# Attention with expert routing beside it: slots of routed tokens placed in six pieces in bodies 5 and 7, in place of three lumps in bodies 4 and 6

## The chip, the cores and the metric

The kernel runs as one program on 1 core of one Trainium2 chip. The metric is the time on the device in microseconds (us); lower is better. Engines: PE is TensorE (matmuls; PEld are its weight loads), DVE is VectorE, ACT is ScalarE, POOL is GpSimd, and SP is the queue of the sync engine, which here starts most of the DMAs.

## The reference, cut to what matters

Eight sequences of 512 tokens with 128 channels pass through six layers.

```python
x = L0_attn_x                                    # (8, 512, 128)
x = x + 0.5 * _L0_ffn_ref(_layernorm(x), ...)    # 8 experts, top 2: phase moe0, first time
x = x + _L0_attn_ref(_layernorm(x), ...)         # phase attn
x = x + 0.5 * _L0_ffn_ref(_layernorm(x), ...)    # moe0, second time
x = x + 0.5 * _L1_ffn_ref(_layernorm(x), ...)    # 16 experts, top 2: moe1
x = x + _L1_attn_ref(_layernorm(x), ...)         # state space: ssm
x = x + 0.5 * _L1_ffn_ref(_layernorm(x), ...)    # moe1

# _L0_attn_ref: 16 heads of 8 channels, softmax over 512 keys
attn = softmax(einsum('bhqd,bhkd->bhqk', q, k) * scale)
out = einsum('bhqk,bhkd->bhqd', attn, v)

# _L0_ffn_ref: which two experts a token goes to
logits = xf @ w_router
topk_w, topk_idx = top_k(softmax(logits), 2)
```

The change is in the attention phase, and in the routing for the mixture behind it, which is worked out beside attention.

## The kernel before

Each engine has its program written out by hand, and semaphores tie them. The phase of attention (`attn_phase`) runs eight *bodies*, one for each sequence b. A body has 16 steps, `st`, each with two *units*; the number of a unit, `at = 2 * st + j`, runs from 0 to 31. In a unit TensorE makes one tile of transposed scores of two heads (`st_pe`, L2227) in a pair of PSUM banks, and ScalarE takes its exponential (`exp_act`, L2235). In the same unit TensorE makes the tile of scores that is 16 units ahead (`max_pe`, L2159), and VectorE takes its maximum over the keys (`max_dve`, L2167). Both kinds of tile go through three PSUM pairs in turn. In each step comes the product with the values too (`av_pe`, L2245).

Other work stands between the units at fixed places, in order on each engine. On VectorE `between_dve` has: outputs divided by their sums (`o_dve`, L2267 and L2269) at units 6, 14, 22 and 30, the residual of the sequence before (`z_dve`, L2297) at 10, statistics for the router at 11 and 12 (L435, L444), v with its bias at 18 (L1911, up to body 5), and up to body 4 eight pieces of the combining of the previous mixture's outputs (L324) and the statistics of a later sequence. On TensorE `turn_pe` has work that shares PSUM bank 7, so that each piece waits until what the one before it left there has been read: among it the projections of q (unit 1, L1812), k (unit 15, L1817) and v (unit 17, L1823) of sequence b + 2, the transposes of the split maxima, `mT_pe` (L2203, units 3, 11, 19 and 27), and the transposes for the norm of sequence b + 3 in the last unit (L1831).

GpSimd (`pool_b`) splits the maxima of four heads into three bf16 parts (`msplit_pool`, L2191 to L2195), which `mT_pe` waits for. It splits q and k of sequence b + 2 (`split_pool`, L1902 to L1906), takes the root for the router's norm (`seq_root`, L451 to L456), starts gathers of the previous mixture's rows (`gather_one`, L277, bodies 0 to 3), and *sends*: indirect DMAs that scatter normalized token rows into the experts' slots in HBM (`group_send`, L635). The pace of these DMAs is a wait on the number of finished exponentials.

The next mixture needs a slot for each token and each of its two experts. This goes by groups: group 0 is sequences 1 and 2, group 1 is 3 and 4, group 2 is 5 and 6. For each, VectorE picks the experts (`pick_a`, `pick_b`), TensorE counts positions (`group_pos`), ScalarE copies them (`group_copy`, L513), and VectorE places (`place_a`, `place_b`, `place_c`). Picking and placing are chains of small operations of 8 to 168 elements a partition, and each waits for the one before it. One table sets where they stand:

```python
late = {"pick_a": (0, 13), "pick_b": (0, 14), "pos": (1, 0), "place_a": (1, 5), "place_b": (1, 6), "place_c": (1, 7)}
GROUP_STEPS = ((3, late), (5, late), (7, last_body))
```

The first number is added to the group's body, the second is the step; `route_dve` runs them at the step's end. So group 0 is picked in steps 13 and 14 of body 3, counted in step 0 of body 4, and placed in units 11, 13 and 15 of body 4; group 1 likewise in bodies 5 and 6. Group 0's 16 sends follow in bodies 4 and 5 and group 1's in 6 and 7, in each body four behind the split of k and four at the end.

## Time and profile before

| what | value |
| --- | --- |
| time, median of 3 runs | 1492.95 us (1492.89 to 1493.4) |
| profiled execution, its own time | 1504.16 us |
| its span, first to last instruction | 1502.4 us |
| PE, DVE, ACT, POOL busy | 1298.2, 1153.1, 888.8, 522.2 us |
| chain that ended last | PE 58%, DVE 22%, issue 8%, ACT 6% |
| attention, first to last exponential | 322.9 to 739.8 us |
| bodies 0, 1, 2, 3 | 50.4, 53.6, 49.7, 52.8 us |
| bodies 4, 5, 6, 7 | 62.3, 50.4, 53.5, 44.2 us |
| L2167, maximum of a tile | 256 of them, mean 1218 ns |
| L2235, exponential of a tile | 256 of them, mean 1022 ns |

A body's length is from its first exponential to that of the next body. The profile is of one execution. Busy matmuls overlap, so a busy TensorE is not one at its peak. The granted clock is a share of 2.4 GHz; TensorE has two levels, 1.2 and 2.4 GHz, so 0.5 means the lower one throughout.

### The profile page before, as it was taken

What the parts mean: (1) busy time and instruction counts of PE and PEld (TensorE: products, weight loads), DVE (VectorE), ACT (ScalarE), POOL (GpSimd) and SP (SyncE); (2) the same over time, 40 slices, a digit from 0 to 9 for tenths busy, and PEclk for the clock granted to TensorE, in tenths of its full rate; (3) what the DMA queues carried; (4) which work ended last, traced back from release to release, by engine and by line L of the source; (5) the groups of instructions that cost most, each with busy time, mean ns of one, the idle gap of its engine ahead of it and who ended that gap; (6) DMA issues with size and microseconds to landing.
All of it is one profiled execution on the core that took longest, in us unless ns stands there. A gap on an engine that the chain in (4) does not pass through costs nothing.

```text
span 1502.4 us, 20416 instructions
## 1 busy us (share of the span) xinstructions
PE 1298.2 (86%) x6496; PEld 777.0 (52%) x6496; DVE 1153.1 (77%) x2430; ACT 888.8 (59%) x1402; POOL 522.2 (35%) x757
## 2 busy tenths in 40 slices
PE   3589999778899879979678999989999889889998
PEld 3467778522222212312256777766666444666665
DVE  5757979789989979898446989878786663787875
ACT  4567667348778858867666677633343465434432
POOL 6664326354534524522243334523430120201100
PEclk9989999869989989989989999999999998999999
DMA  8151264332212202210061122163543011055344
GB/s 298 50 136 61 91 210 148 114 105 84 88 42 88 84 29 75 87 36 23 16 252 50 49 71 91 57 149 92 122 106 79 13 28 25 1 114 115 78 93 113
DMA packets 88679, 133.94 MB, mean 89 GB/s; under 512 B 16756, under 2 KB 42836, under 8 KB 87548
## 3 DMA queue, kind: packets, MB, share of 16 engines
q1 hardware_dynamic: 81404, 117.93, 27.5%
q0 software_dynamic: 7168, 14.69, 3.2%
q8 instruction: 53, 0.87, 0.2%
q14 instruction: 54, 0.44, 0.1%
HBM read 82.23 MB, written 47.45 MB: 86 GB/s over the span
## 4 chain that ended last, share of the span: by engine, by line
PE 58%; DVE 22%; issue 8%; ACT 6%; DMA 3%; SPq 2%; POOL 0%; another core or an unknown queue 0%; DVEq 0%; ACTq 0%; POOLq 0%
PE bank L1557 6%; PE pair L894 5%; DVE shared L2167 5%; PE pair L896 5%; PE pair L895 5%; PE bank L2245 5%; PE pair L1469 3%; PE pair L1471 3%; PE pair L1470 3%; PE pair L2227 3%; PE pair L2159 3%; DVE shared L950 3%; ACT shared L2235 2%; PE bank L964 1%; DMA shared<-p_coef_rows 1%
## 5 line engine op out<-in xcount | busy, mean ns | idle before, releaser
L2167 DVE TENSOR_REDUCE shared<-pair 128x2 f32<-128x1024 f32 x256 | 310.0, 1218 | 45.4 <-PE pair L2159 41.9
L2235 ACT ACTIVATE shared<-pair 128x1024 f32<-128x1024 f32 x256 | 260.6, 1022 | 60.6 <-PE pair L2227 58.3
L950 DVE TENSOR_TENSOR shared<-shared 128x512 fp32r<-128x512 f32 x232 | 195.5, 851 | 91.7 <-ACT shared L940 56.7
L894 PE MATMUL pair<-shared 128*128 128x512 f32 x464 | 201.0, 433 | 12.6 <-issue 8.7
L1524 ACT ACTIVATE shared<-pair 128x512 f32<-128x512 f32 x144 | 85.6, 595 | 179.1 <-PE pair L1471 168.8
L896 PE MATMUL pair<-shared 128*128 128x512 f32 x464 | 189.4, 408 | 0.0
L895 PE MATMUL pair<-shared 128*128 128x512 f32 x464 | 189.0, 407 | 0.0
L935 ACT ACTIVATE shared<-pair,shared 128x512 f32<-128x512 f32 x168 | 115.9, 690 | 74.2 <-PE pair L896 68.6
L1469 PE MATMUL pair<-shared 128*128 128x512 f32 x288 | 153.8, 534 | 5.1 <-DVE shared L1479 5.1
L635 POOL DMA_INDIRECT xs_rows<-shared,slots x112 | 118.2, 1055 | 85.0 <-issue 24.6
L2245 PE MATMUL bank<-shared 128*9 128x512 f32 x1024 | 140.4, 622 | 4.5 <-ACT shared L2235 3.7
L277 POOL DMA_INDIRECT staged<-ys_rows,slots x112 | 118.1, 1054 | 58.9 <-ACT shared L2235 32.3
L1536 DVE TENSOR_TENSOR shared<-shared,pair 128x512 f32<-128x512 f32 x128 | 87.1, 682 | 58.8 <-ACT shared L1524 53.9
L1557 PE MATMUL bank<-shared,down_w 128*128 128x512 f32 x256 | 129.0, 595 | 1.9 <-DVE shared L1545 1.9
L2159 PE MATMUL pair<-shared 48*128 48x512 bf16 x512 | 105.0, 409 | 20.7 <-ACT shared L2235 9.9
L1471 PE MATMUL pair<-shared 128*128 128x512 f32 x288 | 114.9, 399 | 0.0
L1470 PE MATMUL pair<-shared 128*128 128x512 f32 x288 | 114.4, 397 | 0.0
L2227 PE MATMUL pair<-shared 51*128 51x512 bf16 x512 | 103.0, 400 | 12.9 <-DVE shared L2167 11.8
L894 PEld LDWEIGHTS pair<-shared 128*128 128x128 f32 x464 | 92.3, 199 | 32.4 <-issue 14.9
L2227 PEld LDWEIGHTS pair<-shared 51*128 51x128 bf16 x512 | 24.8, 93 | 159.7 <-issue 92.3
L896 PEld LDWEIGHTS pair<-shared 128*128 128x128 f32 x464 | 91.2, 196 | 22.0
L895 PEld LDWEIGHTS pair<-shared 128*128 128x128 f32 x464 | 92.7, 200 | 17.1 <-issue 0.2
(380 smaller groups left out, 2282.0 us busy)
## 6 DMA issues: line engine op xcount, KB each, us to landing
shared<-p_coef_rows SPq DMA_DIRECT2D x64, 512.0 KB
shared<-xs_rows SPq DMA_DIRECT2D x42, 256.0 KB
ys_rows<-shared SPq DMA_DIRECT2D x42, 256.0 KB
w_keep<-shared SPq DMA_DIRECT2D x8, 1024.0 KB
shared<-w_keep SPq DMA_DIRECT2D x16, 512.0 KB
shared<-p_q_parts SPq DMA_DIRECT2D x64, 96.0 KB
shared<-p_k_parts SPq DMA_DIRECT2D x64, 96.0 KB
xs_rows<-shared SPq DMA_DIRECT2D x1, 5376.0 KB, 18.4
```

Source lines behind the costliest of these rows:

```text
L894: nc.tensor.matmul(out_bank, w_hi, x_hi, start=start, stop=False)
L895: nc.tensor.matmul(out_bank, w_hi, x_lo, start=False, stop=False)
L896: return nc.tensor.matmul(out_bank, w_lo, x_hi, start=False, stop=stop)
L950: nc.vector.tensor_tensor(hl[u % RING][:], hid[u % RING][:], hh[u % RING][:], ALU.subtract).then_inc(s["dve_done"], 1)
L1469: nc.tensor.matmul(out_bank, w_hi, x_hi, start=start, stop=False)
L1470: nc.tensor.matmul(out_bank, w_hi, x_lo, start=False, stop=False)
L1471: return nc.tensor.matmul(out_bank, w_lo, x_hi, start=False, stop=stop)
L1557: nc.tensor.matmul(bank[6][:], w, h, start=(j == 0), stop=(j == IT - 1)).then_inc(s["down_done"], 1)
L2167: nc.vector.tensor_reduce(mneg[:, i, 2 * c:2 * c + 2], pair_of("max", b, m)[:], AX_X, ALU.max, negate=True).then_inc(s["mx_read"], 1)
L2227: last = nc.tensor.matmul(pair_of("exp", b, 2 * st + p)[:, f, :], ka[par][rows, c, kt * P:(kt + 1) * P], qa[par][rows, c, :], start=True, ...
L2235: nc.scalar.activation(probs[st % 2][:, 2 * p:2 * p + 2, :], pair_of("exp", b, 2 * st + p)[:], ACT.Exp, scale=scale).then_inc(s["exp_done" ...
L2245: last = nc.tensor.matmul(bank[6][32 * hh:32 * hh + HD + 1, :], v_all[:, b * TILES + kt, hh % 2 * (H // 2) + g * HG // 2 + hh // 2, :], pr ...
```

## The change

Placing moves to body 5 (group 0) and body 7 (group 1), into the first third of the body, in six pieces: `place_a`, `place_b` and `place_c` get an argument `half`, and `between_dve` runs the halves at units 3, 4, 5, 7, 8 and 9. Picks and counts come one body later. The sends of group 0 are spread over bodies 5 and 6 in twos, those of group 1 over body 7 in fours, at new places in GpSimd's order. Group 2 and the last sequence stay as they were. The lists of step names (`PE_STEPS`, `ACT_STEPS`, `DVE_STEPS`), from which the values of the waits are counted, follow the new order.

```diff
-        def place_a(v, occ, G):
+        def place_a(v, occ, G, half=None):
...
+            if half == 0:
+                return
             before = upto_e[1 - G % 2][:, NE0 - 1:NE0] if G else 0.0
...
-        def place_b(v, occ, G):
+        def place_b(v, occ, G, half=None):
...
+            if half == 0:
+                return
             chain(nc.vector.tensor_tensor(q, r, s1, ALU.mult))
...
-        def place_c(v, occ, G):
+        def place_c(v, occ, G, half=None):
...
+            if half == 0:
+                return
             chain(nc.vector.tensor_tensor(past_e[:], upto_e[G % 2][:].unsqueeze(1).to_broadcast([P, NBLK, NE0]),
...
-            late = {"pick_a": (0, 13), "pick_b": (0, 14), "pos": (1, 0), "place_a": (1, 5), "place_b": (1, 6), "place_c": (1, 7)}
+            late = {"pick_a": (0, 13), "pick_b": (0, 14), "pos": (1, 0)}
+            PLACED_IN = {5: 0, 7: 1}
+            PLACE_AT = {3: (place_a, 0), 4: (place_a, 1), 5: (place_b, 0), 7: (place_b, 1), 8: (place_c, 0), 9: (place_c, 1)}
...
-            GROUP_STEPS = ((3, late), (5, late), (7, last_body))
+            GROUP_STEPS = ((4, late), (6, late), (7, last_body))
...
+                if routed and b in PLACED_IN and at in PLACE_AT:
+                    place, half = PLACE_AT[at]
+                    place(v, routes, PLACED_IN[b], half)
                 if routed and at == 11:
...
-                sends = routes is not None and b > 3
-
-                def send(half):
-                    group_send(g, routes, (b - 4) // 2, 2 * (b % 2) + half, 4, lambda k, n: paced(b, 4 * half + k, 8))
+
+                def send(G, part, parts, at, every):
+                    if routes is not None:
+                        group_send(g, routes, G, part, parts, lambda k, n: g.wait_ge(s["exp_done"], PER * b + min(PER, int(at + every * k))))
...
+                if b == 6:
+                    send(0, 4, 8, 2, 2)
                 msplit_pool(g, b, 2)
                 fetch((3, 9))
                 xbo_pool(b)
                 if routes is not None and b:
                     seq_root(g, routes, b - 1)
                 fetch((4, 12))
+                if b == 5:
+                    send(0, 0, 8, 10, 1)
+                if b == 6:
+                    send(0, 5, 8, 11, 2)
+                if b == 7:
+                    send(1, 0, 4, 10, 1.5)
                 if b + FIRST < B:
                     split_pool(g, "q", b + FIRST)
                 fetch((5, 15))
+                if b == 5:
+                    send(0, 1, 8, 14, 1)
                 msplit_pool(g, b, 3)
                 if b + FIRST < B:
                     split_pool(g, "k", b + FIRST)
                 fetch((6, 20))
-                if sends:
-                    send(0)
+                if b == 5:
+                    send(0, 2, 8, 20, 2)
+                if b == 6:
+                    send(0, 6, 8, 18, 2)
+                if b == 7:
+                    for part in range(1, 4):
+                        send(1, part, 4, 12 + 5 * part, 1.25)
                 if not last_:
                     msplit_pool(g, b + 1, 0)
                 if b + AHEAD < B:
                     shift_a(f0 + b + AHEAD)
                 fetch((7, 27))
-                if sends:
-                    send(1)
+                if b == 5:
+                    send(0, 3, 8, 27, 2)
+                if b == 6:
+                    send(0, 7, 8, 27, 2)
```

Lines have other numbers after the change: the maximum L2167 is L2179, `o_dve` L2267 and L2269 are L2279 and L2281, `place_b` L598 to L606 is L603 to L613, `split_pool` L1902 to L1906 is L1912 to L1916, `msplit_pool` L2191 to L2195 is L2203 to L2207, and a send, L635, is L645.

VectorE, body 4 before, units 13 and 14: `place_b` of group 0 in one lump between two maxima (L2167), behind a piece of the combining (L324).

```order
L2167 TENSOR_REDUCE shared<-pair 128x2
L324 SCALAR_TENSOR_TENSOR x_res<-staged,w_tok,x_res 128x128
L598 TENSOR_TENSOR q_g<-pos_g,room_e 128x64
L599 TENSOR_TENSOR q_g<-q_g,jump_e 128x64
L600 TENSOR_TENSOR r_g<-pos_g,next_e 128x64
L601 TENSOR_TENSOR r_g<-r_g,q_g 128x64
L602 TENSOR_TENSOR q_g<-r_g,s_g 128x64
L603 TENSOR_REDUCE slot_f<-q_g 128x8
L604 TENSOR_TENSOR q_g<-r_g,sel_all 128x64
L605 TENSOR_REDUCE slot_f<-q_g 128x8
L606 CAST slots<-slot_f 128x16
L2167 TENSOR_REDUCE shared<-pair 128x2
```

VectorE, body 5 after, units 4 to 7: the end of `place_a`, the maximum of unit 5 (L2179), and `place_b` in two halves, with two maxima and `o_dve` between them.

```order
L593 TENSOR_TENSOR jump_e<-jump_e,next_e 128x8
L2179 TENSOR_REDUCE shared<-pair 128x2
L603 TENSOR_TENSOR q_g<-pos_g,room_e 128x64
L604 TENSOR_TENSOR q_g<-q_g,jump_e 128x64
L605 TENSOR_TENSOR r_g<-pos_g,next_e 128x64
L606 TENSOR_TENSOR r_g<-r_g,q_g 128x64
L2179 TENSOR_REDUCE shared<-pair 128x2
L2279 RECIPROCAL shared<-bank 128x16
L2281 TENSOR_TENSOR shared<-bank,shared 128x4x32
L2179 TENSOR_REDUCE shared<-pair 128x2
L609 TENSOR_TENSOR q_g<-r_g,s_g 128x64
L610 TENSOR_REDUCE slot_f<-q_g 128x8
```

The lump of nine operations has become a piece of four and one of five (the last three of it stand behind these rows), and it stands eight units earlier in the next body.

GpSimd, body 5 before, behind the statistics of unit 12: the end of `seq_root` (L456), the split of q, the maximum split of the body's last four heads, and the start of the split of k.

```order
L456 TENSOR_TENSOR sh_all<-sh_all,rs_all 128x4
L1902 CAST shared<-shared 128x512
L1903 TENSOR_TENSOR shared<-shared 128x512
L1904 CAST shared<-shared 128x512
L1906 TENSOR_TENSOR shared<-shared 128x512
L2191 CAST shared<-shared 128x8x2
L2192 TENSOR_TENSOR shared<-shared 128x16
L2193 CAST shared<-shared 128x8x2
L2195 TENSOR_TENSOR shared<-shared 128x8x2
L1902 CAST shared<-shared 128x512
```

GpSimd, body 5 after, the same place (L645 is a send):

```order
L456 TENSOR_TENSOR sh_all<-sh_all,rs_all 128x4
L645 DMA xs_rows<-shared,slots 10752x128 x2
L1912 CAST shared<-shared 128x512
L1913 TENSOR_TENSOR shared<-shared 128x512
L1914 CAST shared<-shared 128x512
L1916 TENSOR_TENSOR shared<-shared 128x512
L645 DMA xs_rows<-shared,slots 10752x128 x2
L2203 CAST shared<-shared 128x8x2
L2204 TENSOR_TENSOR shared<-shared 128x16
L2205 CAST shared<-shared 128x8x2
L2207 TENSOR_TENSOR shared<-shared 128x8x2
L1912 CAST shared<-shared 128x512
```

Two sends have come between `seq_root` and the split of q, and two more between that and the maximum split.

GpSimd, body 7 before: the end of `seq_root`, the maximum split of the last four heads, and eight sends.

```order
L456 TENSOR_TENSOR sh_all<-sh_all,rs_all 128x4
L2191 CAST shared<-shared 128x8x2
L2192 TENSOR_TENSOR shared<-shared 128x16
L2193 CAST shared<-shared 128x8x2
L2195 TENSOR_TENSOR shared<-shared 128x8x2
L635 DMA xs_rows<-shared,slots 10752x128 x8
```

GpSimd, body 7 after, the same place:

```order
L456 TENSOR_TENSOR sh_all<-sh_all,rs_all 128x4
L645 DMA xs_rows<-shared,slots 10752x128 x4
L2203 CAST shared<-shared 128x8x2
L2204 TENSOR_TENSOR shared<-shared 128x16
L2205 CAST shared<-shared 128x8x2
L2207 TENSOR_TENSOR shared<-shared 128x8x2
L645 DMA xs_rows<-shared,slots 10752x128 x12
```

Four sends now stand ahead of the maximum split, and twelve behind it.

## Rows read from the trace of the kernel before

**Rows 1.** Stretches, L2235 alone: span, length, busy (instructions), granted clock, DMA; units 12 to 19.

```profile
444.70:457.80 13.10, 8.18 (x9) 1.00 0.30 97
551.50:573.30 21.80, 8.21 (x9) 0.84 0.19 59
609.40:622.20 12.80, 8.18 (x8) 1.00 0.31 94
660.70:678.80 18.10, 8.18 (x8) 0.81 0.09 30
```

**Rows 2.** Stretches, L2235 alone: last units of bodies 2, 3; first units of 2, 4.

```profile
470.90:476.60 5.70, 4.01 (x4) 1.00 0.26 83
520.60:529.40 8.80, 4.03 (x4) 0.87 0.18 54
426.90:432.80 5.90, 4.10 (x5) 1.00 0.04 11
529.40:539.60 10.20, 4.10 (x4) 0.61 0.01 2
```

**Rows 3.** Stretches of VectorE: place_a (body 4), the lumps (body 6), units 3 to 9.

```profile
552.44:554.29 1.85, 1.43 (x11) 1.00 0.10 14
...
661.57:663.08 1.51, 1.27 (x9) 1.00 0.03 8
665.61:667.96 2.35, 2.04 (x10) 1.00 0.00 0
670.72:672.69 1.97, 1.70 (x9) 0.50 0.00 0
596.37:606.65 10.28, 8.93 (x9) 1.00 0.15 41
700.82:711.14 10.32, 8.93 (x10) 1.00 0.01 3
```

**Rows 4.** Timeline of bodies 4 and 6: start, length, engine, line, operation, [idle before <-releaser].

```profile
558.56 1.15 POOL L1903 TENSOR_TENSOR shared<-shared 128x512 f32<-128x512 f32 x1
558.59 1.20 DVE L602 TENSOR_TENSOR q_g<-r_g,s_g 128x64 f32<-128x64 f32 x1
...
666.73 0.22 DVE L602 TENSOR_TENSOR q_g<-r_g,s_g 128x64 f32<-128x64 f32 x1
```

**Rows 5.** Timeline of TensorE, bodies 4, 5, 6 and 7.

```profile
555.57 0.39 PE L2227 MATMUL pair<-shared 51*128 51x512 bf16 x2 [1.90 <-DVE shared L2167]
...
563.46 2.08 PE L1817 MATMUL bank<-xnT,w_k 128*128 128x512 f32 x2 [5.76 <-DVE shared L2269]
...
614.58 1.12 PE L1817 MATMUL bank<-xnT,w_k 128*128 128x512 f32 x2 [0.79 <-DVE shared L2269]
...
617.72 1.16 PE L1823 MATMUL bank<-w_v,xnT 128*128 128x128 f32 x8
...
621.33 0.39 PE L2203 MATMUL bank<-identb,shared 128*12 128x128 bf16 x4 [0.40 <-DVE shared L1911]
...
669.33 0.39 PE L2227 MATMUL pair<-shared 51*128 51x512 bf16 x2 [2.85 <-DVE shared L2167]
...
723.14 0.39 PE L2203 MATMUL bank<-identb,shared 128*12 128x128 bf16 x4
```

**Rows 6.** Timeline of GpSimd, bodies 5 and 7.

```profile
613.71 0.20 POOL L456 TENSOR_TENSOR sh_all<-sh_all,rs_all 128x4 f32<-128x4 f32 x1
...
617.55 0.21 POOL L2191 CAST shared<-shared 128x16 bf16<-128x16 f32 x1
...
618.41 0.22 POOL L2195 TENSOR_TENSOR shared<-shared 128x16 bf16<-128x16 f32 x1
...
622.51 1.12 POOL L635 DMA_INDIRECT xs_rows<-shared,slots  x1 [0.17 <-issue]
623.93 0.97 POOL L635 DMA_INDIRECT xs_rows<-shared,slots  x1 [0.30 <-issue]
...
718.18 0.20 POOL L456 TENSOR_TENSOR sh_all<-sh_all,rs_all 128x4 f32<-128x4 f32 x1
```

More of the change, by code:

```diff
@@ L568, in pick_dense @@
             v.wait_ge(rs_["dve_step"], dve_at(occ, "pkd"))
-        def place_a(v, occ, G):
+        def place_a(v, occ, G, half=None):
             ts, nt, b = group(occ, G)
             chain = route_chain(v)
-            v.wait_ge(rs_["act_step"], act_at(occ, f"p{G}"))
+            if half != 1:
+                v.wait_ge(rs_["act_step"], act_at(occ, f"p{G}"))
             counts = pos_g[:, NE0 * nt:NE0 * (nt + 1)]
             upto = upto_e[G % 2]
-            if G == 0:
+            if G == 0 and half != 1:
                 chain(nc.vector.memset(next_e[:], 0.0))
@@ L613, in place_c @@
             counts = pos_g[:, NE0 * nt:NE0 * (nt + 1)]
-            chain(nc.vector.scalar_tensor_tensor(out=moved_e[:], in0=rest_e[:], scalar=0.0, in1=jump_e[:], op0=ALU.is_gt, op1=ALU.mult))
-            chain(nc.vector.tensor_tensor(next_e[:], next_e[:], counts, ALU.add))
-            chain(nc.vector.tensor_tensor(next_e[:], next_e[:], moved_e[:], ALU.add))
-            chain(nc.vector.scalar_tensor_tensor(out=room_e[:], in0=blocks_e[:], scalar=float(T), in1=rest_e[:], op0=ALU.mult, op1=ALU.subtract))
+            if half != 1:
+                chain(nc.vector.scalar_tensor_tensor(out=moved_e[:], in0=rest_e[:], scalar=0.0, in1=jump_e[:], op0=ALU.is_gt, op1=ALU.mult))
+                chain(nc.vector.tensor_tensor(next_e[:], next_e[:], counts, ALU.add))
+                chain(nc.vector.tensor_tensor(next_e[:], next_e[:], moved_e[:], ALU.add))
+                chain(nc.vector.scalar_tensor_tensor(out=room_e[:], in0=blocks_e[:], scalar=float(T), in1=rest_e[:], op0=ALU.mult, op1=ALU.subtract))
+            if half == 0:
+                return
             chain(nc.vector.tensor_tensor(past_e[:], upto_e[G % 2][:].unsqueeze(1).to_broadcast([P, NBLK, NE0]),
```

26 lines of the change are left out of this document (13 added, 13 removed).

## The prediction

> **What bounds the kernel now.** I read the busy shares and the chain of waits on the page first, then the stages of the attention phase cut at its Exp instructions, then the timeline inside them. "Body b" is the loop body of attention that computes the scores of sequence b; its 32 "units" are its 32 Exp instructions, and beside unit u VectorE reduces a maximum 16 units ahead (L2167, 1.22 us each, in the table of the profile). An Exp tile and a maximum tile share three PSUM pairs, so when VectorE is late, the tile of a later Exp is late too. ScalarE has slack. In a body without routing work the chain of waits alternates between TensorE and VectorE, and neither has much to give: eight units or nine take 11 to 13 us.
>
> The small routing work is what breaks the rhythm. Units 12 to 19 take 13.1 us in body 2, which has no placing, and 21.8 us in body 4, where the lumps of group 0 stand at units 11, 13 and 15 [rows 1]. That is 8.7 us of excess. For group 1 in body 6 the same units take 18.1 us. Body 6 projects no k and v; body 5 does, and takes 12.8 us. Of that the k projection (1.12 us on TensorE [rows 5]) certainly falls away and the v projection (1.16 us) partly, so the base of body 6 is 10.5 to 11.7 us; I take 11.1, and the excess is 7.0 us. The picks with the position counts behind them cost too: the last four units of body 3 take 8.8 us against 5.7 in body 2, and the first four of body 4 take 10.2 against 5.9 [rows 2], together 7.4 us.
>
> **What the lumps are made of.** The three lumps last 1.51, 2.35 and 1.97 us in body 6 [rows 3], 5.83 us in sum. In body 4 place_a takes 1.85 us (it has three memsets more). Its place_b is slower than body 6's, since single operations are stretched: L602 takes 1.20 us there, with GpSimd's L1903 of the split of q running at the same moment, and 0.22 us in body 6, where no split runs [rows 4]. The Trainium skill, GPSIMD Engine Reference, section Key points, says that GpSimd shares its SBUF interfaces with VectorE and contends with VectorE instructions that have two SBUF inputs. The trace agrees (1.20 against 0.22 us). By that rule units 3 to 9, where only the four short operations of a maximum split run on GpSimd, are free of it, which is also what I assume from the rows. So in the new place group 0 costs 1.85 + 2.35 + 1.97 = 6.17 us and group 1 5.83 us of VectorE. The rest of the excess is idle TensorE: gaps of 5.76 us in body 4 and 2.85 us in body 6, and after each a stretch in which TensorE runs at its lower clock (1.2 GHz): k's pair of matmuls takes 2.08 us where body 5 needs 1.12 [rows 5].
>
> **Part 1: the lumps go.** Saved: 8.7 (body 4) + 7.0 (body 6) = 15.7 us.
>
> **Part 2: six pieces in units 3, 4, 5, 7, 8, 9 of bodies 5 and 7.** From the maximum of unit 3 to that of unit 10 VectorE is busy 8.93 of 10.28 us in body 5 and 8.93 of 10.32 us in body 7 [rows 3], so 1.35 and 1.39 us are free. No piece is longer than 1.25 us, so a piece goes into a gap and the buffer behind it, not in front of a standing TensorE. But 6.17 us of work go into 1.35 us of room: slip 6.17 - 1.35 = 4.8 us in body 5 and 5.83 - 1.39 = 4.4 us in body 7. Directly behind follow z_dve, the statistics and their aggregation (units 10 to 12), where VectorE has no idle time to catch up. Bounds: 0 (all of it beside TensorE, which is what the chain runs through up to unit 9) and 12.0 us for both (none hidden). I stay with 9.2, since in bodies 4 and 6 nothing of the lumps was hidden.
>
> **Part 3: the sends.** A send is one indirect DMA on GpSimd's queue, about 1.12 us for the first and 0.97 for the next with 0.30 between [rows 6]. Their number is the same (32), but what stands behind them is not. In body 5 two sends now stand between seq_root and the split of q, and two more between that and the maximum split of group 3 (see the order of GpSimd's instructions). That split feeds mT(5,3), which TensorE takes up in unit 19, in order. Today seq_root ends at 613.91, the split of q follows without a gap, the maximum split ends at 618.63, and TensorE starts the transposes at 621.33, having waited 0.40 us for VectorE: 2.7 us of room [rows 5, 6]. Each pair of sends adds 0.17 + 1.12 + 0.30 + 0.97 = 2.56 us, two pairs 5.1. All four are past their pace by then (Exp 10, 11, 14, 15 are done). So the split ends at 623.75 and TensorE stands 2.4 us longer. Queued behind on TensorE are all later Exp and maximum tiles, so ScalarE and VectorE stand too. Behind the split on GpSimd stand the split of k, two sends and the next maximum split, which has some 5 us until its maximum is read; nobody waits there. In body 7 four sends stand between seq_root (ends 718.38) and the maximum split: 718.38 + 0.17 + 1.12 + 3 x 0.30 + 3 x 0.97 = 723.5, and 1.08 for the split (617.55 to 618.63 in body 5) gives 724.6, against transposes that start at 723.14 today: 1.4 us. In body 6 two sends stand there; the split has to wait for its maximum about as long anyway: 0. Sum 3.8 us, bounds 0 and 4.
>
> **Part 4: clock.** TensorE's clock fell after idle 5.76 and 2.85 us but not after the single 1.90 us [rows 5]. In body 5 the gap in unit 19 would be 0.40 + 2.4 = 2.8 us, so I expect a short fall there: the work behind it (Exp, maximum and AV tiles, about 0.9 us a unit at 2.4 GHz) doubles for a few units that have half a microsecond of room each; I take 1.0 us, and 0.3 in body 7, where the gap is shorter. Bounds 0 and 6.4: at worst the clock is low from the pieces on, and the 4.9 us of TensorE on body 5's chain from k to the tiles of unit 19 double, with 1.5 us in body 7.
>
> **Part 5: picks and positions move one body on.** Group 0's go from the end of body 3 and start of body 4 to the end of 4 and start of 5. The norm transposes behind the pick (b + 3 < 8) and the q projection behind the positions (b + 2 < 8) are there too, so the 7.4 us move and stay. Group 1's go from bodies 5/6 to 6/7, neither of which has those. I price it at 0, with 1 us to both sides. The fillers of body 4 that the old sends stood among gain nothing, since no engine waits for those. The last send is due at Exp 30 as before, so the MoE phase behind starts unchanged.
>
> **Sum.** -15.7 + 9.2 + 3.8 + 1.3 = -1.4 us. The profiled execution took 1504.16 us (span 1502.4), which is 11.2 us more than the median of the timed runs, 1492.95; the excess lies on all phases, so I carry the difference over unchanged: 1491.5 us.
>
> **Rivals.**
> 1. GpSimd isn't late. If the sends cost its queue less than their rows, or if the pieces' slip leaves the statistics no later while v of unit 18 is, the 3.8 us and the clock's 1.3 go: -6.5 us, 1486.5. For it: today one gather stands at each of the two places in bodies 0 to 3, and nobody waits. Against it: 2.7 us of room hold one pair, not two.
> 2. The slip is not hidden at all (12.0), all else as forecast: +1.4 us, 1494.3, no measurable change. For it: the lumps were paid in full. Against it: 1.35 us of idle time are in the rows.
> 3. Slower, by one mechanism: TensorE's clock. Pieces between all maxima thin out TensorE from unit 3 on; if the clock falls there and is still low when k and v are projected in units 15 to 17, 6.4 us stand in place of 1.3: +3.7 us, 1496.6. It decides from about 3 us of low clock on TensorE's part of the chain. For it: 0.61 was granted in the first units of body 4 [rows 2], right before where the pieces now would be in body 5. Against it: in bodies 4 and 6 it came back as soon as the lumps were over.
> 4. The same work in the same amounts is merely moved, and each place costs what the old one did: 0.
>
> **Chances.** Forecast 0.42, rival 1 0.25, rival 2 and 4 together 0.18, rival 3 0.15. A measurement of this kernel tells about 0.2% (3 us) from no change, that is 1490.0 and 1495.9. Faster: rival 1 nearly whole (0.23) and a third of the forecast's spread (0.13), 0.36. Slower: most of rival 3 (0.12) and tails of the rest (0.10), 0.22. Within: 0.42. Range: from rival 1 to rival 3, 1486.5 to 1496.6; beside it, the forecast's own is 1489 to 1494.
>
> **What would show it.** In the profile after: units 12 to 19 of bodies 4 and 6 back near 13.1 and 11.1 us; units 3 to 10 longer by 4.8 and 4.4 us in bodies 5 and 7, with VectorE without idle time and pieces at their uncontended durations; a wait of TensorE of about 2.8 us before the transposes of unit 19 in body 5, released by GpSimd, and one of 1.4 us in body 7; an end of body 4 and a start of body 5 like those of 3 and 4 before. No wait there means rival 1; k at 2.08 us in body 5 means rival 3. I am wrong altogether if places that I call unchanged (body 3, or what follows attention) move by more than 1 us.

## The result: no gain where a small one was forecast, and slower in the first measurement

| kernel | median us | runs | ratio to before | 95% interval |
|---|---|---|---|---|
| changed, first measurement | 1506.9 (before 1492.95) | 5 | 1.0093 | 1.0055 to 1.0131 |
| changed, again | 1496.65 | 12 | 1.0012 | 0.9985 to 1.0039 |
| changed, third time | 1498.72 | 12 | 1.0019 | 0.9985 to 1.0053 |

The forecast was 1491.5 us, range 1486.5 to 1496.6. The first measurement is 15 us above it, and the other two lie at the upper end of the range and above it. They put the kernel 2.5 and 4.8 us above the medians of before that were taken beside them (1494.16 and 1493.95), which the ratios can't tell from none. The ratios leave out single slow runs (one, of kernel 7 below, took 2446 us) and are not quotients of the medians. Otherwise a kernel's runs spread over 9 to 26 us, so the lengths of the bodies in the traces are the sharper measure. Those below repeat within 2 us for one kernel; in the pieces-only kernel body 4 differed by 2.8 us between two profiles. Most of that lies in the first three units behind group 0's picks, which take 5.7 to 8.9 us and differ by 2 to 3 us between profiles of one kernel; the units behind them are steadier. I read the bodies as before, from Exp to Exp (L2247 now; other lines of attention have moved by 10 or 12 too: the maximum is L2179, AV L2257, mT's transposes L2215, the split's last operation L2207, a send L645).

| us | body 3 | 4 | 5 | 6 | 7 | sum |
|---|---|---|---|---|---|---|
| before, first and second profile | 52.8, 52.2 | 62.3, 60.5 | 50.4, 50.4 | 53.5, 52.7 | 44.2, 44.2 | 263.2, 260.0 |
| changed, three profiles | 49.7, 49.7, 49.7 | 51.8, 51.4, 52.0 | 60.4, 60.4, 61.1 | 49.1, 49.1, 49.1 | 55.2, 56.4, 56.6 | 266.2, 267.0, 268.5 |

The change takes 10 us from body 4 and 4 from body 6 and puts 10 us on body 5 and 11 to 12 on body 7. The stretches that answer to [rows 1] and [rows 2], ScalarE's L2247 alone (stretch, length, busy (instructions), granted clock, DMA share, GB/s): units 12 to 19 of bodies 2, 4 and 6; units 19 to 21 of body 5 and 22 to 31 of body 7; the last units of body 4 and first of 5, and the last of body 3.

```profile
442.80:455.90 13.10, 8.20 (x9) 1.00 0.32 99
542.10:555.20 13.10, 8.17 (x8) 1.00 0.30 93
654.90:666.30 11.40, 8.16 (x8) 1.00 0.17 54
...
612.30:622.30 10.00, 3.07 (x3) 0.67 0.45 138
722.90:740.80 17.90, 10.05 (x10) 0.71 0.11 37
567.50:576.20 8.70, 4.03 (x5) 0.92 0.16 48
576.20:584.40 8.20, 4.07 (x4) 0.88 0.00 0
518.60:524.40 5.80, 4.05 (x5) 1.00 0.29 83
```

Body 4 reads like body 2, and body 6 needs 11.4 us where it needed 18.1. The picks' 19.0 us of two stretches [rows 2] have moved by one body and take 16.9, with a higher clock in the second. That is no gain of the change: the first four units behind the picks took 10.2 and 8.3 us in the two profiles of before (body 4) and 8.3, 9.5 and 10.3 us in the three after it (body 5). VectorE in units 3 to 11 of bodies 5 and 7, which took 13.3 us before (see [rows 3] for units 3 to 9):

```profile
583.00:601.00 18.00, 16.47 (x39) 0.91 0.09 23
690.10:708.30 18.20, 16.31 (x36) 0.81 0.01 2
```

It is busy 92% and 90% of the time, and the units take 17.9 and 18.2 us. TensorE does wait for VectorE here, as in unit 7 of body 5, and its clock falls for a while (0.91 and 0.81 granted over the two stretches):

```profile
591.59 0.89 PE L2288 MATMUL bank<-ident,shared 128*128 128x128 f32 x4 [2.22 <-DVE shared L2281]
```

The waits that answer to [rows 5]: TensorE in unit 19 of body 5 and what follows (start, us, engine, line, operation, [idle before <-releaser]).

```profile
612.12 0.38 PE L2171 MATMUL pair<-shared 48*128 48x512 bf16 x2
616.29 0.59 PE L2215 MATMUL bank<-identb,shared 128*12 128x128 bf16 x4 [3.79 <-POOL shared L2207]
...
617.78 1.90 PE L2257 MATMUL bank<-shared 128*9 128x512 f32 x8
```

TensorE waits 3.79 us for GpSimd's split, and at its lower clock (1.2 GHz; 0.67 granted over the three units) an AV tile then takes 1.90 us instead of 1.05. Now body 7, which holds the larger part of the miss. GpSimd first, from the split for unit 19 on (compare [rows 6]), then ScalarE, then TensorE:

```profile
719.03 0.22 POOL L2207 TENSOR_TENSOR shared<-shared 128x16 bf16<-128x16 f32 x1
719.74 1.01 POOL L645 DMA_INDIRECT xs_rows<-shared,slots  x1 [0.49 <-issue]
721.05 0.96 POOL L645 DMA_INDIRECT xs_rows<-shared,slots  x1 [0.30 <-issue]
722.32 0.96 POOL L645 DMA_INDIRECT xs_rows<-shared,slots  x1 [0.30 <-issue]
...
728.62 0.96 POOL L645 DMA_INDIRECT xs_rows<-shared,slots  x1 [0.31 <-issue]
```

```profile
725.87 1.03 ACT L2247 ACTIVATE shared<-pair 128x1024 f32<-128x1024 f32 x1
728.97 0.58 ACT L2264 COPY shared<-bank 128x512 f32<-128x512 f32 x1 [2.06 <-remote]
729.71 1.02 ACT L2247 ACTIVATE shared<-pair 128x1024 f32<-128x1024 f32 x1 [0.15 <-remote]
```

```profile
719.39 0.38 PE L2215 MATMUL bank<-identb,shared 128*12 128x128 bf16 x4 [1.83 <-POOL shared L2207]
...
725.13 1.05 PE L2257 MATMUL bank<-shared 128*9 128x512 f32 x8 [0.21 <-ACT shared L2247]
...
727.42 0.39 PE L2239 MATMUL pair<-shared 51*128 51x512 bf16 x2
730.78 1.90 PE L2257 MATMUL bank<-shared 128*9 128x512 f32 x8 [2.97 <-issue]
```

Eight sends stand in one row, 1.26 us from start to start (six in the two later profiles). ScalarE's L2264 wants the AV tile, which TensorE had done at 726.18 by the trace; it starts at 728.97, and the trace names no releaser ("remote"). TensorE waits for ScalarE in turn, and its clock falls. Units 22 to 31 take 18.0 us against 12.5 before. What the late signal is, the experiments had to say.

### The profile page after: what moved, and what is told of

The parts are those of the page before. It is cut to its first block, busy times and chain, and to the rows that moved or that the text cites. A ratio compares the mean times of both kernels' runs of the same rounds, so it can differ in the third digit from the quotient of the medians.

```text
span 1503.5 us, 20427 instructions
## 1 busy us (share of the span) xinstructions
PE 1293.0 (86%) x6496; PEld 775.9 (52%) x6496; DVE 1152.8 (77%) x2430; ACT 887.5 (59%) x1402; POOL 523.1 (35%) x757
## 4 chain that ended last, share of the span: by engine, by line
PE 54%; DVE 23%; issue 9%; ACT 7%; DMA 3%; SPq 2%; POOL 2%; another core or an unknown queue 1%; DVEq 0%; POOLq 0%; ACTq 0%
PE bank L1567 6%; PE pair L904 5%; PE pair L905 5%; PE pair L906 5%; PE bank L2257 5%; DVE shared L2179 5%; PE pair L1479 3%; PE pair L1481 3%; PE pair L1480 3%; PE pair L2239 3%; DVE shared L960 3%; PE pair L2171 3%; ACT shared L2247 2%; DMA shared<-p_coef_rows 1%; PE bank L974 1%
## 5 line engine op out<-in xcount | busy, mean ns | idle before, releaser
L2179 DVE TENSOR_REDUCE shared<-pair 128x2 f32<-128x1024 f32 x256 | 310.0, 1218 | 41.7 <-PE pair L2171 37.7
L2247 ACT ACTIVATE shared<-pair 128x1024 f32<-128x1024 f32 x256 | 260.3, 1021 | 55.9 <-PE pair L2239 52.2
L904 PE MATMUL pair<-shared 128*128 128x512 f32 x464 | 199.0, 429 | 11.2 <-issue 7.2
L905 PE MATMUL pair<-shared 128*128 128x512 f32 x464 | 187.6, 404 | 0.0
L645 POOL DMA_INDIRECT xs_rows<-shared,slots x112 | 119.0, 1063 | 79.3 <-issue 27.5
L2257 PE MATMUL bank<-shared 128*9 128x512 f32 x1024 | 140.8, 623 | 6.4 <-ACT shared L2247 3.3
L2171 PE MATMUL pair<-shared 48*128 48x512 bf16 x512 | 103.8, 403 | 22.3 <-ACT shared L2247 11.4
L1481 PE MATMUL pair<-shared 128*128 128x512 f32 x288 | 116.4, 404 | 0.0
L904 PEld LDWEIGHTS pair<-shared 128*128 128x128 f32 x464 | 91.3, 197 | 30.4 <-issue 13.2
L906 PEld LDWEIGHTS pair<-shared 128*128 128x128 f32 x464 | 90.6, 195 | 21.5
L905 PEld LDWEIGHTS pair<-shared 128*128 128x128 f32 x464 | 91.2, 197 | 16.7 <-issue 0.2
```

What stands on the lines that cost most here:

```text
L904: nc.tensor.matmul(out_bank, w_hi, x_hi, start=start, stop=False)
L905: nc.tensor.matmul(out_bank, w_hi, x_lo, start=False, stop=False)
L906: return nc.tensor.matmul(out_bank, w_lo, x_hi, start=False, stop=stop)
L1481: return nc.tensor.matmul(out_bank, w_lo, x_hi, start=False, stop=stop)
L2179: nc.vector.tensor_reduce(mneg[:, i, 2 * c:2 * c + 2], pair_of("max", b, m)[:], AX_X, ALU.max, negate=True).then_inc(s["mx_read"], 1)
L2247: nc.scalar.activation(probs[st % 2][:, 2 * p:2 * p + 2, :], pair_of("exp", b, 2 * st + p)[:], ACT.Exp, scale=scale).then_inc(s["exp_done" ...
```

## The experiments

All lines in the expectations count from the kernel they name. Each kernel was timed in 12 runs (one in 11), beside before on the same chip.

**1 and 2. Both kernels again.** No edit.

> The kernel before, unchanged, run against itself. It says how far two executions of one kernel lie apart, since the profiled execution of before took 1504.16 us and its timed runs 1490 to 1498. If the 14 us of the change are its own (theory 1), this ratio is 1.000 within 0.3% and its runs lie near 1493. If both kernels have a wide and common spread and the change only drew the worse part of it (theory 2), some of these runs lie at 1500 and above. In the profile I expect bodies 2, 3, 4, 5, 6, 7 of 49.7, 52.8, 62.3, 50.4, 53.5, 44.2 us again within 0.5 us where the clock is the same.

> The changed kernel, unchanged, as the reference of this group. Theory 1: ratio 1.007 to 1.011 again (about 1504 to 1509 us against 1493). Theory 2: a ratio under 1.005, since the attention phase of the one profile is only some 3 us longer than before's where the clock is alike. Both expect in the profile a wait of TensorE for GpSimd of 3 to 4 us in unit 19 of body 5 and 1.5 to 2 us in unit 19 of body 7.

Before took 1492.66 us, ratio 1.0018 to itself (0.9982 to 1.0053); the changed kernel took 1496.65, as theory 2 has it. The 14 us between the medians of the first measurement did not return. The bodies of the changed kernel did, and both waits of unit 19 (3.79 and 1.83 us). Those of before returned less well than the 0.5 us I expected: body 4 took 60.5 us instead of 62.3, body 6 52.7 instead of 53.5, and body 1, which the change does not touch, 49.7 instead of 53.6. The two profiles that belong to the first measurement are only 1.1 us apart in span (1502.4 and 1503.5 us), so no stretch of them can show the rest.

**3. The pieces alone.** The pieces in units 3 to 9 of bodies 4 and 6; picks, positions and sends as before.

```
-            late = {... "pos": (1, 0), "place_a": (1, 5), "place_b": (1, 6), "place_c": (1, 7)}
+            late = {"pick_a": (0, 13), "pick_b": (0, 14), "pos": (1, 0)}
+            PLACED_IN = {4: 0, 6: 1}
```

> One part of the change alone: the six pieces in units 3, 4, 5, 7, 8, 9, but in the old bodies 4 and 6, with the old picks, counts and sends. If the pieces are what is good in the change and the new places of the sends are what is bad (my account), bodies 4 and 6 get shorter by 3.9 and 2.6 us (8.7 and 7.0 of lumps go, 4.8 and 4.4 of slip come), nothing waits for GpSimd, and the time is 4 to 8 us under before's: 1485 to 1489, ratio 0.995 to 0.997. The rival, that pieces between all maxima cost more than lumps (TensorE's clock, or turns of bank 7 that wait for late VectorE), expects 1493 or more and units 3 to 12 of bodies 4 and 6 longer by over 8 us.

Measured 1489.2 us, ratio 0.9983 (0.9949 to 1.0017). Body 4 went from 60.5 us (before, second profile) to 56.5 and body 6 from 52.7 to 51.1. Run once more, unchanged:

> The kernel with the pieces only, unchanged, once more, to narrow its ratio (0.9983 of before, 0.9949 to 1.0017, the first time). If its bodies 4 and 6 gain 5.6 us as their lengths say, the ratio is 0.996 to 0.998; if that is given back elsewhere, 1.000.

1489.42 us, ratio 0.9969 (0.9947 to 0.9991). Here the bodies were 59.3 and 51.9 us, so the 5.6 us of the first profile did not return whole. Without the three units behind the picks the gain is steady: units 3 to 31 take 50.8 and 50.5 us in body 4, where before needs 53.5 and 53.6, and 45.8 and 46.0 us in body 6, where before needs 48.2 and 48.3. So six pieces do beat three lumps where the lumps stood, and the loss of the change is not in them.

**4. The sends of bodies 5 and 7 behind the split for unit 19.** The same calls ahead of the split are removed.

```
                 msplit_pool(g, b, 3)
...
                 fetch((6, 20))
                 if b == 5:
+                    send(0, 0, 8, 10, 1)
+                    send(0, 1, 8, 14, 1)
                     send(0, 2, 8, 20, 2)
...
                 if b == 7:
+                    send(1, 0, 4, 10, 1.5)
                     for part in range(1, 4):
```

> The changed kernel with the sends that stood ahead of the maximum split of unit 19 (four in body 5, four in body 7) put right behind it (body 5: behind the split of k), nothing else. My account: the waits of TensorE for GpSimd in unit 19 of bodies 5 and 7 (3.8 and 1.8 us) go with the fall of the clock behind the first, so attention is 5 to 8 us shorter than with the change, 1496 to 1502 us if the change takes 1507 here. If the long row of back-to-back sends in body 7 is what costs (its 16 sends now all come after unit 18, without a gap), units 20 to 31 of body 7 get longer than the 22.6 us they take with the change, and the gain is under 3 us. Rival, that the time is lost outside attention: no change against the changed kernel.

The gain did not come: 1504.78 us, ratio 1.0079 (1.0048 to 1.0109). Unit 19 did fall to 1.49 us in body 5 and 1.37 in body 7, as it should, but body 5 took 61.8 us and body 7 60.2. That is the second branch of the expectation, the long row: units 20 to 31 of body 7 took 25.6 us (20.6 in the changed kernel, not the 22.6 given there). The sends now stood in rows of six (615.0 to 621.5) and eleven (717.9 to 730.7). ScalarE in the second row:

```profile
724.42 1.02 ACT L2247 ACTIVATE shared<-pair 128x1024 f32<-128x1024 f32 x1 [0.88 <-PE pair L2239]
727.96 1.02 ACT L2247 ACTIVATE shared<-pair 128x1024 f32<-128x1024 f32 x1 [2.52 <-remote]
730.07 0.59 ACT L487 COPY shared<-bank 128x512 f32<-128x512 f32 x1 [1.08 <-remote]
731.54 1.02 ACT L2247 ACTIVATE shared<-pair 128x1024 f32<-128x1024 f32 x1 [0.89 <-PE pair L2239]
735.07 0.59 ACT L2264 COPY shared<-bank 128x512 f32<-128x512 f32 x1 [2.50 <-remote]
```

The Exp at 727.96 reads scores that TensorE had ready at 725.48. The trace also records when a semaphore is raised. Over attention that is 0.02 us after the end of TensorE's instruction in the median of 742. Here the score tile's signal is recorded at 727.93, 2.45 us late, and ScalarE starts 0.03 us after it; the AV tile done at 730.08 is signalled at 735.05, and ScalarE starts at 735.07. In body 5's row VectorE waits so too (1.43 and 1.69 us, "remote"). Hence theory A of the experiments that follow: in a row of sends the signals of other engines come late. Its rival B: an instruction fetch, or waits for mT. The traces speak against a fetch. In the changed kernel's first profile the nearest one of 16 KB lies ahead of the row, from 716.34 to 717.87, and none is recorded between 719.2 and 741 us in this one.

**5. The kernel before, with the eight sends of body 7 in one row.** Nothing else moves: same number of sends, same order on GpSimd.

```
-                nc.gpsimd.wait_ge(s["exp_done"], PER * b + 16 + 16 * k // n)
+                nc.gpsimd.wait_ge(s["exp_done"], PER * b + (20 if b == B - 1 else 16 + 16 * k // n))
```

> The kernel before, with one change: the eight sends of body 7 are all let go at unit 20 instead of two units apart, so that they stand in one row on GpSimd, some 1.27 us from start to start (before: 2.3 to 2.8 us apart; body 7 took 44.2 us in both profiles of this kernel). Theory A (late signals): while sends follow each other at 1.27 us, from the third or fourth on, TensorE's signals reach ScalarE late, as in the kernel with sends behind the split (ScalarE idle 2.52, 1.08 and 2.50 us 'remote' in a row of eleven). Eight in a row should then cost body 7 2 to 6 us: 46 to 50 us, with ScalarE waits put down to 'remote' of 0.5 us and more. Rival B (what was seen there was an instruction fetch or the waits for mT, and a row of sends costs the other engines nothing): body 7 stays at 44.2 within 0.5 us and no such wait appears; the sends then just end 5 us earlier. The time: A 1492.7 + 4 = 1497, B 1492.7.

1502.03 us, ratio 1.0054 (1.0029 to 1.0079). Body 7 went from 44.2 to 51.6 us, more than the 46 to 50 I gave theory A, and rival B falls. GpSimd, ScalarE, TensorE (its Exp is L2235, scores L2227, AV L2245):

```profile
723.55 1.12 POOL L635 DMA_INDIRECT xs_rows<-shared,slots  x1 [3.90 <-ACT shared L2235]
724.98 0.97 POOL L635 DMA_INDIRECT xs_rows<-shared,slots  x1 [0.30 <-issue]
...
732.57 0.96 POOL L635 DMA_INDIRECT xs_rows<-shared,slots  x1 [0.31 <-issue]
```

```profile
729.52 1.02 ACT L2235 ACTIVATE shared<-pair 128x1024 f32<-128x1024 f32 x1 [0.89 <-PE pair L2227]
732.38 0.59 ACT L2252 COPY shared<-bank 128x512 f32<-128x512 f32 x1 [1.84 <-remote]
733.79 1.02 ACT L2235 ACTIVATE shared<-pair 128x1024 f32<-128x1024 f32 x1 [0.83 <-remote]
```

```profile
727.94 1.04 PE L2245 MATMUL bank<-shared 128*9 128x512 f32 x8 [0.21 <-ACT shared L2235]
...
730.23 0.39 PE L2227 MATMUL pair<-shared 51*128 51x512 bf16 x2
734.87 1.89 PE L2245 MATMUL bank<-shared 128*9 128x512 f32 x8 [4.26 <-issue]
```

The signals are late from the fourth send on: 1.7 us for the score tile done at 727.73, 3.4 us for the AV tile done at 728.98. Up to the row the body is as before. The two stretches, up to unit 22 and from it on, all engines (PE, PEld, DVE, ACT, POOL busy (instructions), granted clock, DMA):

```profile
694.00:725.70 31.70, 26.97 (x204) 7.89 (x208) 22.75 (x32) 26.60 (x35) 7.35 (x19) 1.00 0.01 4
725.70:745.60 19.90, 13.84 (x77) 3.56 (x69) 3.73 (x15) 11.40 (x15) 6.01 (x7) 0.74 0.07 23
```

And the second of them in the repeat of before, where the sends stand 2.3 to 3.0 us apart:

```profile
717.30:729.80 12.50, 10.18 (x77) 3.21 (x69) 3.75 (x15) 10.86 (x15) 4.81 (x5) 1.00 0.08 27
```

The same 77 groups of matmuls take 3.7 us more at the lower clock, and the waits make up the rest of 7.4 us. The DMA engines are no busier than 8% in either. "Done" is the end that the trace gives, and ends of matmuls are modelled; but TensorE started its scores at 730.23, 2.1 us before the signal of the AV tile that it had finished ahead of them.

**6. The pieces alone, with gaps between the sends.** In bodies 4 and 5 the first four sends were due before GpSimd came to them and ran as a row of four, and so did the last four of body 4.

```
-                nc.gpsimd.wait_ge(s["exp_done"], PER * b + 16 + 16 * k // n)
+                nc.gpsimd.wait_ge(s["exp_done"], PER * b + (16 + 2 * k if b == B - 1 else min(PER, 20 + 2 * k)))
```

> The kernel with the pieces only (bodies 4 and 6, old sends), with the sends of bodies 4, 5 and 6 let go at units 20, 22, 24, 26, 28, 30, 32, 32 instead of 16, 18, 20, ... 30: there the first four were due before GpSimd came to them and ran in a row of four, 1.27 us apart (at 561.9, 575.3 and 612.4 us). Theory A (late signals in rows of sends): units 22 and 23 of body 5 come down from 1.94 and 1.96 to 1.6 each or less, body 4's units 19 and 22 from 2.20 and 2.38 to 1.6; bodies 4 and 5 together 106.9 -> 104 to 105.5 us, time 1489.2 -> 1487.5 (less than the measurement can tell). Rival B (rows cost nothing): these units as they are, and the time the same. If later sends hold up the next body's GpSimd work, body 5 or 6 gets longer by 1 to 3 us at its first units: that would be seen at units 0 to 3.

1487.99 us, ratio 0.9963 (0.9934 to 0.9991). Units 22 and 23 of body 5 fell from 1.94 and 1.96 to 1.50 and 1.65, as theory A has it, and unit 22 of body 4 from 2.38 to 1.51. Unit 19 of body 4 stayed at 2.21, so it had nothing to do with the sends, and unit 27 rose from 1.78 to 2.94. Bodies 4 and 5 together did not get shorter: 108.8 us against 106.9, with 2.4 us more in the first three units of body 4, ahead of all sends. In the second profile of kernel 3 they took 109.6 us, so this is the spread of those units. A row of four costs under 1 us, and the time does not show it.

**7. Four sends in body 5, twelve in body 6.**

```
                 msplit_pool(g, b, 3)
...
                 if b == 5:
-                    send(0, 2, 8, 20, 2)
+                    send(0, 0, 8, 21, 2)
...
                 if b == 5:
-                    send(0, 3, 8, 27, 2)
+                    send(0, 1, 8, 27, 2)
```

(and the first two calls in body 5 are gone; body 6 sends parts 2 to 7 in pairs from units 2, 8, 12, 19, 23 and 27.)

> The changed kernel with only four of group 0's sends in body 5 (at units 21, 23, 27, 29, all behind the split of the maxima for unit 19) and twelve in body 6, in pairs two units apart (it had eight and eight, four of them ahead of that split). Theory A (the four sends ahead of the split made mT late, the clock fell after it, and moving them behind it failed only because six then stood in a row): unit 19 of body 5 goes 5.19 -> 1.49, units 20 and 21 2.48 to 2.73 -> 1.36 and to 1.31, body 5 60.4 -> 55 to 56 us, body 6 49.1 -> 49 to 50; time 1496.65 -> 1491.5. Rival B (the work of twelve sends holds up GpSimd's splits in body 6 as it did in body 5): body 6 49.1 -> 52 or more, with waits for L2207 in front of TensorE, and the time stays at 1494 to 1497. Rival C (body 5 is long for the clock alone): body 5 stays at 58 or more.

1495.1 us, ratio 1.0003 (0.9977 to 1.0028), above the 1491.5 that theory A gave. The lengths follow theory A: units 19 to 21 took 4.15 us (as in before; 10.0 in the changed kernel), body 5 55.6, body 6 49.6. Body 7, untouched, took 57.4. TensorE's wait before mT is back to 0.41 us, for VectorE:

```profile
608.99 0.39 PE L2215 MATMUL bank<-identb,shared 128*12 128x128 bf16 x4 [0.41 <-DVE shared L1921]
```

**8. Eight sends in body 7, eight behind it.**

```
-                    send(1, 0, 4, 10, 1.5)
+                    send(1, 0, 8, 10, 2)
...
-                        send(1, part, 4, 12 + 5 * part, 1.25)
+                        send(1, part, 8, 16 + 4 * part, 2)
...
+                if b == 7:
+                    send(1, 1, 2, 32, 0)
```

> The changed kernel with only eight of group 1's sixteen sends in body 7, two units apart and six of them behind the split for unit 19; the other eight follow in a row after body 7's last exponential. Theory A (in body 7 the row of sends makes TensorE's signals late, and sends ahead of the split make mT late): unit 19 2.60 to 2.92 -> 1.37, units 22 to 29 lose the 4 to 5 us that they had over before; body 7 55.2 to 56.4 -> 49 to 51 us (44.2 before, and the pieces' slip of 5). Rival B (these units are slow for an instruction fetch that comes there anyway, or for the clock): body 7 stays at 53 or more. The eight sends in a row stand then where other work runs: what the stretch behind body 7 (to 830 us) pays is 0 if GpSimd is free there and up to 8 x 1.27 = 10 us if not; so the time is 1496.65 - 5.5 + (0 to 10) = 1491 to 1501, and only the body's length decides between A and B.

1496.13 us, ratio 0.9988 (0.9959 to 1.0018): alone, the mend of 7 us in body 7 does not show in the time beyond its noise. Body 7 took 49.0 us: unit 19 is 1.37 and units 22 to 31 take 12.5 us, exactly as before the change; what stays is the pieces' slip. GpSimd in two places:

```profile
722.63 1.01 POOL L645 DMA_INDIRECT xs_rows<-shared,slots  x1 [4.15 <-ACT shared L2247]
724.76 0.96 POOL L645 DMA_INDIRECT xs_rows<-shared,slots  x1 [1.12 <-ACT shared L2247]
...
746.88 0.96 POOL L645 DMA_INDIRECT xs_rows<-shared,slots  x1 [0.30 <-issue]
750.46 0.25 POOL L451 TENSOR_SCALAR sh_all<-mv_all 128x4 f32<-128x4 f32 x1 [2.62 <-DVE mv_all L430]
```

The row behind the body ends 2.6 us before GpSimd is wanted, and from the last Exp to the first matmul of L905 in the next stage it is 17.4 us, against 17.0. To the hundredth matmul of L904 it is 119.2 us, where kernels without such a row take 116.6 to 118.3.

**9. Both mends together** (7 and 8).

> The changed kernel with both edits of its sends at once: four of group 0's sends in body 5 behind the split, twelve in body 6; eight of group 1's in body 7 two units apart, eight behind its last exponential. Theory A (late signals in rows of sends, and sends ahead of the split, are what the changed kernel loses beyond the pieces' slip, and they add up): body 5 55.6 us, body 6 49.6, body 7 49.0, so that bodies 5 to 7 are 11 us shorter than in the second run of the changed kernel (165.9 -> 154 to 156), and the stretch behind pays nothing; time 1496.65 - 6 to 11 = 1486 to 1491. Rival B (what is gained there comes back as a lower clock elsewhere, as the runs of single mends gained only 1.6 and 0.5 us in the median): bodies 154 to 156, but the time stays at 1494 to 1497.

1487.17 us, ratio 0.9953 (0.9924 to 0.9982): faster than before and than the changed kernel. Bodies 5, 6 and 7 by stretch:

```profile
577.00:630.30 53.30, 45.93 (x327) 14.29 (x325) 46.44 (x77) 40.09 (x51) 17.32 (x33) 0.97 0.20 63
630.30:679.90 49.60, 41.82 (x314) 12.65 (x314) 44.28 (x63) 38.65 (x49) 18.19 (x33) 1.00 0.14 45
679.90:728.60 48.70, 40.11 (x280) 10.98 (x278) 31.23 (x71) 37.83 (x48) 13.41 (x25) 0.93 0.04 12
```

and in the changed kernel:

```profile
576.20:636.60 60.40, 49.62 (x327) 14.37 (x325) 46.55 (x77) 40.29 (x51) 20.90 (x36) 0.90 0.20 61
636.60:685.70 49.10, 41.96 (x314) 12.70 (x315) 44.28 (x63) 38.55 (x49) 14.29 (x29) 1.00 0.13 39
685.70:740.80 55.10, 43.11 (x280) 12.40 (x278) 31.09 (x71) 38.16 (x48) 21.03 (x33) 0.85 0.06 20
```

151.6 us against 164.6, with the same work on every engine but GpSimd (one weight load more or less in the records), and the time follows (rival B said it would not): the changed kernel beside it took 1498.72 us. Body 5 is shorter here than the 55.6 us expected because its first three units took 5.7 us, 8.1 in kernel 7; 1.1 of the 13 us between the two tables are of that kind.

**10. Group 1 placed where VectorE has no maxima.** Kernel 3, with group 1's pieces in units 17 to 22 of body 7 and its sends from unit 26 on, most of them behind the body.

```
+            PLACE_AT = {4: dict(zip((3, 4, 5, 7, 8, 9), HALVES)), 7: dict(zip((17, 18, 19, 20, 21, 22), HALVES))}
...
+                    group_send(g, routes, 1, pace=lambda k, n: g.wait_ge(s["exp_done"], PER * b + min(PER, 26 + 2 * k)))
```

> The kernel with the pieces only, but group 1's six pieces in body 7 at units 17 to 22, where VectorE has no maxima left to find, in place of body 6 at units 3 to 9; group 1's sends two units apart from unit 26 of body 7, most of the sixteen in a row behind its last exponential. Theory A (the slip of 5 us is VectorE's queue alone, so pieces cost nothing where no maximum stands behind them): body 6 51.1 -> 49 to 49.6, body 7 44.2 -> 44.2 to 45.5, stretch behind it (last exponential to the first matmul of the next stage 17.1 us) as before; time 1489.2 -> 1487.5. Rival B (twelve sends behind the last exponential hold up the next stage's own sends and its first loads of routed rows): that stretch grows by up to 12 x 1.27 = 15 us, and the time goes to 1495 to 1504. Rival C (VectorE is wanted there after all, by the picks and the copies of the last body): body 7 goes to 47 or more.

1486.12 us, the lowest median of all, ratio 0.9968 (0.9937 to 0.9999). Body 6 took 46.9 us (51.1 in kernel 3) and body 7 stayed at 44.2:

```profile
633.30:680.20 46.90, 43.28 (x315) 12.67 (x313) 41.97 (x50) 38.68 (x48) 6.32 (x21) 0.96 0.09 27
680.20:724.40 44.20, 37.10 (x277) 11.09 (x277) 31.43 (x71) 37.45 (x48) 8.53 (x20) 1.00 0.02 6
```

Body 6 is below the 49 to 49.6 us I expected; it lost its sends with its pieces, but its units 3 to 11 alone went from 17.5 us to 13.3, which is the whole difference. Pieces cost nothing where no maximum stands behind them in VectorE's queue, so the slip is that queue. From the last Exp to the first matmul of L905 it stays at 17.1 us; the hundredth matmul of L904 comes 120.4 us behind the last Exp, 117.3 in kernel 3. In kernel 9, with eight sends in that place, it is 116.4. Whether this or kernel 9 is the better one the intervals don't tell.

**11. The changed kernel a third time.**

> The changed kernel, unchanged, a third time (1.0093 the first time, 1.0012 the second). By the bodies of its two profiles (bodies 4 to 7 take 6 to 7 us more than before) it should be at 1.003 to 1.006; if the first measurement held for all chips, 1.009; if the second, 1.001.

1498.72 us, ratio 1.0019 (0.9985 to 1.0053), with the same bodies as in the first two profiles. It came between the expectation from the second measurement and that from the bodies.

## Why the prediction was wrong

By its own parts, in the profile that belongs to it:

| part | forecast | measured | how |
|---|---|---|---|
| 1, lumps go | -8.7, -7.0 | -8.7, -6.7 | units 12 to 19: 21.8 to 13.1, 18.1 to 11.4 |
| 2, pieces' slip | +4.8, +4.4 | +4.6, +4.8 | units 3 to 11: 13.3 to 17.9 and 18.2 |
| 3 and 4, unit 19 of body 5 and the clock | +2.4, +1.0 | +5.9 (repeats +4.8, +4.9) | units 19 to 21: 4.15 to 10.0 |
| 3 and 4, unit 19 of body 7 | +1.4, +0.3 | +1.2 (repeats, with unit 20, +2.5, +2.3) | 1.37 to 2.60; wait 1.83 us |
| not priced: row of sends in body 7 | 0 | +5.5 (repeats +5.0, +5.6) | units 22 to 31: 12.5 to 18.0 |
| 5, picks and positions | 0 | -2 in this pair, none shown | 19.0 to 16.9 us; repeats of either kernel differ by 2 |

**Parts 1 and 2 held in size.** The lumps were paid in full, and the slip is the pieces' work minus VectorE's free time. One sentence of part 2 did not hold: pieces were not to stand "in front of a standing TensorE", but TensorE waited 2.22 us there and its clock fell, which part 4 had not in its sum. That is the first half of rival 3; the slip came within 0.4 us of its forecast even so. For the rule on shared interfaces (the Trainium skill, GPSIMD Engine Reference, section Key points) the new place agrees too: L609, the operation that was L602, takes 0.21 us there, where no long operation of GpSimd runs beside it. Experiment 10 shows the price is a matter of the queue, not of the pieces.

**The step that failed is in part 3.** "Their number is the same (32), but what stands behind them is not" looked only at who is queued behind the sends on GpSimd, and priced those ahead of the split; part 5 added when the last is due. Neither asked how closely the rest follow. Group 1's slots come in body 7 now, so sixteen sends share what is left of one body where eight were, and GpSimd, which seq_root and the split hold up, catches up in a row of eight at 1.26 us (six in the repeats). That row makes TensorE's signals late, and the idle time drops the clock. Experiment 5 makes the same loss out of the kernel before with nothing but the row (+7.4 us), 4 makes it worse with a longer one, and in 8, where eight sends are spread and eight moved out, it is gone to the last tenth. It is 5.0 to 5.6 of the 11 to 12 us of body 7; the slip and unit 19 are the rest.

**Unit 19 of body 5 was mis-sized.** The mechanism was right: the wait stands where forecast and GpSimd is its releaser, and experiment 7 removes all of it. But it was 3.79 us, not 2.8: the sends' own gaps were 0.56 and 0.77 us where I had taken 0.17 and 0.30 from [rows 6]. The low clock lasted to 622.5 and cost 5.9 - (3.8 - 0.4) = 2.5 us in the first profile, about 1.5 in the others, against 1.0. Together with body 7's row that is 6.5 to 8 us, and turns the forecast of -1.4 into +5 to +6.5 for bodies 3 to 7; the pairs of profiles show +3.0 and +7.0. Rival 3, the slower one, had another mechanism: the clock was not low where k and v are projected in body 5 (units 12 to 18 took 11.3 us, as before).

**The sign that the prediction gave itself.** It called itself wrong altogether if body 3 or what follows attention moved by more than 1 us. Body 3 did, by 2.5 to 3.1 us. But part 5 had itself moved the picks out of its last units, so this sign contradicted the sum and says nothing against it. What follows attention took 762.6 us in before's first profile and 762.7 in the changed kernel's, and 750.3 to 763.8 over all profiles, so 1 us can't be read there.

**What stays open.** The ratio of 1.0093 in the first measurement is more than these 5 us (0.3%); two later ones do not have it. I can't say what it was. The changed kernel's first profile is 9.5 us longer than its second, and 8.2 of these lie behind attention (762.7 against 754.5 us), where the change has nothing; but before's profiles reach 762.6 there too. Nor do the runs show by what way sends hold up other engines' signals, or whether the signal alone or the finished tile with it comes late. The semaphore records are themselves incomplete there: sends 2 us and more apart leave all 16 signals of their landings in the trace of kernel 8 (724.72 to 724.90 for the send of 722.63), those in the row of experiment 5 leave 1 to 6 of 16. So a single late record could be a lost one; that ScalarE starts within 0.03 us of the record, again and again, and that the timed runs follow in kernels 4, 5 and 9, is what speaks for the delay itself.

## What to carry to other kernels

When work is moved, count what it sends behind it, and over how much time: an indirect DMA that waits for nobody is still not free if eight of them catch up in one row. Pace such sends two units (2.3 to 3.0 us here) apart, or put them in a row where no engine hands work to another closely; with 8 or 13 of them behind the last Exp the hundredth matmul of the next stage came 116.4 to 120.4 us behind it, where it is 116.6 to 118.3 without. And put small VectorE work where its queue has slack behind it, not merely small gaps: the same pieces cost 5 us among the maxima and nothing behind the last one.

## What the runs showed of the hardware

- In rows of six and more sends, 1.26 us apart, signals of TensorE arrived up to 5.0 us after its work by the trace, against 0.02 us in the median. In kernel 5 the 16 DMA engines were 7% busy meanwhile. A row of four cost 0.3 and 0.4 us in two units of one body and 0.9 in one of another. In the profile this looks like ScalarE or VectorE waiting for "remote" and TensorE for "issue", with GpSimd, which causes it, named nowhere.
- A send's row on GpSimd ends before its data have landed: the send of 722.63 in kernel 8 ended at 723.64, and its landings signalled at 724.72 to 724.90. The Trainium skill, Perfetto Trace Analysis, section DMA Instruction — SWDGE (GPSIMD), says that the row ends when the descriptors are written and not when the data are moved; the trace agrees, and at 1.26 us from start to start two sends are under way at once.
- The clock of TensorE did not follow the length of one wait alone. Behind the wait of 3.79 to 3.81 us in unit 19 of body 5 the lower one (0.5) was granted for 6.8 us in the first profile and for 3.4 us in the repeats; behind the 1.83 us of body 7 it fell in the repeats (an AV tile then took 1.90 us) and not in the first.
- The spread of one kernel's runs, 9 to 26 us, is as large as all that was tried here; medians of 12 runs still moved by up to 2 us between measurements. Units 3 to 31 of a body repeat far better than its first three behind the picks.
